# Norm statistics by ScalarE's accumulator, and step sizes whose logarithm stays in PSUM

## The reference

```python
h = _layernorm(x, axis=-1) * (1 + ca) + sa
x = x + ga * _L0_attn_ref(h, ...)        # inside: a second layernorm of h, with a scale and a bias
h = _layernorm(x, axis=-1) * (1 + cb) + sb
x = x + gb * _L0_ffn_ref(h, ...)

# _L0_attn_ref, its core
xn = (x - mu) * rsqrt(var + 1e-05) * norm_scale + norm_bias
xb, z = split(xn @ W_in)
xb = silu(conv3(xb) + conv_b)
dt = softplus(xb @ W_dt + b_dt)
h = exp(dt * A) * h + (dt * x_t) * B_t       # per token, 16 states of 512 channels
y_t = sum_n(h * C_t)
return residual + ((y + D * xb) * silu(z)) @ W_out
```

## Time and profile before

| | us |
|---|---|
| median of three runs | 3125.44 |
| lowest and highest | 3113.62, 3128.53 |
| the profiled execution | 3116.45 |
| its span | 3114.7 |
| a row in the middle of it | 181.1 |
| DVE busy, share of the span | 2638.9, 85% |
| POOL busy | 2623.7, 84% |
| PE busy | 2564.0, 82% |
| ACT busy | 1313.1, 42% |

### The profile page before, as it was taken

How to read it: one execution, slowest core, us unless ns; L and a number is a source line. 1 busy time by engine, 2 the same in 40 slices (tenths; PEclk the granted TensorE clock), 3 DMA queues, 4 the chain that set the end, 5 groups by cost and what they waited for, 6 DMA issues and landing times.

```text
span 3114.7 us, 29047 instructions
## 1 busy us (share of the span) xinstructions
PE 2564.0 (82%) x9260; PEld 1772.5 (57%) x9260; DVE 2638.9 (85%) x3121; ACT 1313.1 (42%) x2081; POOL 2623.7 (84%) x1354
## 2 busy tenths in 40 slices
PE   3435796988979798897979899797988879798879
PEld 1112574656657465665756566574656657465668
DVE  2589898998989899898989998898989989898932
ACT  1434453444445344444534444354444445444311
POOL 0499898989989898998988899898989989898922
PEclk8767898999989898998989899898989989898989
DMA  5234343444434343444434344444434434443411
GB/s 148 75 114 124 120 136 109 130 130 126 146 120 132 114 134 126 131 141 121 136 114 131 124 137 136 119 136 124 132 119 134 133 119 136 122 132 122 149 42 50
DMA packets 282074, 383.40 MB, mean 123 GB/s; under 512 B 44080, under 2 KB 146992, under 8 KB 281920
## 3 DMA queue, kind: packets, MB, share of 16 engines
q1 hardware_dynamic: 281920, 381.54, 40.3%
HBM read 371.38 MB, written 10.06 MB: 122 GB/s over the span
## 4 chain that ended last, share of the span: by engine, by line
PE 33%; POOL 27%; DVE 20%; issue 15%; ACT 4%; SPq 1%; DMA 1%; POOLq 0%; DVEq 0%; ACTq 0%
PE wbank L450 10%; POOL unit L1094 9%; PE mbank L462 6%; DVE hbank L740 5%; POOL act L1082 4%; PE wbank L368 4%; DVE unit L747 4%; PE wbank L478 3%; PE wbank L406 3%; POOL gsum L1114 3%; POOL unit L1109 3%; POOL gsum L1109 2%; DVE st L537 2%; PE wbank L392 2%; POOL dtx L1061 1%
## 5 line engine op out<-in xcount | busy, mean ns | idle before, releaser
L1094 POOL TENSOR_TENSOR unit<-dtx,b_bc 128x1024 f32<-128x1024 f32 x512 | 1213.0, 2371 | 3.6 <-DMA b_bc<-bc_scratch 3.6
L740 DVE TENSOR_TENSOR_SCAN hbank<-hbank,unit 128x1024 f32<-128x1024 f32 x512 | 1172.2, 2290 | 26.0 <-POOL unit L1094 25.5
L973 ACT ACTIVATE hbank<-dt,a_neg 128x512 f32<-128x512 f32 x1024 | 666.6, 681 | 532.3 <-DVE unit L747 484.1
L450 PE MATMUL wbank<-h_t,up_t 128*128 128x256 f32 x2048 | 540.3, 411 | 138.2 <-DVE act L712 68.5
L747 DVE TENSOR_TENSOR unit<-hbank,c_bc 128x1024 f32<-128x1024 f32 x512 | 622.7, 1216 | 18.5 <-DMA c_bc<-bc_scratch 0.7
L450 PEld LDWEIGHTS wbank<-h_t,up_t 128*128 128x128 f32 x2048 | 411.5, 205 | 262.8 <-DVE act L712 74.5
L450 PE MATMUL wbank<-h_t,gate_t 128*128 128x256 f32 x2048 | 519.4, 400 | 48.8 <-DVE gz L594 48.5
L462 PE MATMUL mbank<-down_t,act 128*128 128x256 f32 x2048 | 511.4, 389 | 43.5 <-POOL act L1082 43.3
L1082 POOL TENSOR_TENSOR act<-act,w_all 128x512 f32<-128x512 f32 x256 | 337.3, 1318 | 199.1 <-DVE act L719 199.1
L462 PEld LDWEIGHTS mbank<-down_t,act 128*128 128x128 f32 x2048 | 390.3, 194 | 166.6 <-POOL act L1082 73.4
L450 PEld LDWEIGHTS wbank<-h_t,gate_t 128*128 128x128 f32 x2048 | 411.1, 202 | 115.4 <-DVE gz L594 52.8
(11 more groups left out here) (120 smaller groups left out, 2353.7 us busy)
## 6 DMA issues: line engine op xcount, KB each, us to landing
b_bc<-bc_scratch SPq DMA_DIRECT2D x512, 256.0 KB, 4.4
c_bc<-bc_scratch SPq DMA_DIRECT2D x512, 256.0 KB, 4.3
w_all<-w_scratch SPq DMA_DIRECT2D x256, 256.0 KB, 3.5
ht<-in_L_attn_x_dram SPq DMA_DIRECT2D x16, 512.0 KB, 5.0
xt<-in_L_attn_x_dram SPq DMA_DIRECT2D x16, 512.0 KB, 4.9
out_dram<-xt SPq DMA_DIRECT2D x16, 512.0 KB, 3.3
z<-mod_scratch SPq DMA_DIRECT2D x16, 256.0 KB, 3.4
gsum<-in_L_ffn_gate_proj_dram SPq DMA_DIRECT2D x4, 512.0 KB, 4.3
```

The costliest lines, as they stand in the source:

```text
L450: m = eng.matmul(t.bank[:, j * HT:(j + 1) * HT], w[:, 2 * first + j, k, :], h2_t[:, k, h * HT:(h + 1) * HT], start=k == 0, stop=k == HK - 1)
L740: eng.tensor_tensor_scan(h, h, unit[:, g % RING, :, :].rearrange("p a t -> p (a t)"), 0.0, ALU.mult, ALU.add).then_inc(scanned, 1)
L973: eng.activation(hbank[g % HB][:, a, :], dt[:, 2 * q + a, :], ACT.Exp, scale=a_neg[:, 2 * q + a, n:n + 1]).then_inc(decayed, 1)
L1094: eng.tensor_tensor(unit[:, g % RING, :, :], dtx[:, 2 * q:2 * q + 2, :], b_bc[:, s:s + 1, :].to_broadcast([P, 2, T]), ALU.mult).then_inc(d ...
```

## The change

**Norms.** `norm_stats` goes from DVE. ACT reads the four tiles of a row once with Identity and its accumulator, which gives four sums (`row_sums`; the tile is written back over itself), POOL makes minus the mean of them (`row_means`), ACT reads the tiles again with Square, the bias minus the mean and the accumulator (`row_squares`; the squares themselves go into two tiles of `z2` by turns and are not used), and POOL makes `ve` with one more TENSOR_SCALAR ahead of rstd and shift. A norm thus has eight more ACTIVATE, all with the accumulator, 384 in the 48 norms, and POOL has 96 more TENSOR_SCALAR of 128x4. From DVE go 192 BN_STATS, 192 BN_AGGR and 96 TENSOR_SCALAR. In a norm work now goes ACT, POOL, ACT, POOL, ACT, where it went DVE, POOL, ACT.

**Step sizes.** ACT takes relu into `dt`, then |v|, Exp and Ln in the PSUM bank itself, tile by tile; DVE adds `dt` and the bank per tile (64 of 128x512 where there were 32 of 128x1024) and only that frees the bank. Table loads go from 65 to 129.

**The table.** Stages are cut into other numbers of steps and stand at other moments: `stats` one moment later, `norms` 25 to 37 in 12 steps, `gates` 25 to 42 instead of 19 to 35, `turn_in` from 42, `step_sizes1` 3 to 14 instead of 0 to 5, `mix1` 11 to 12.

```diff
-                plan += [("mix1", behind, 4, 8, 11), ("load_res", behind, 1, 11, 13), ("load_gb", behind, 1, 11, 19),
-                         ("project", behind, 4, 15, 19), ("stats", behind, 4, 18, 19),
-                         ("turn", behind, 4, 23, 27), ("pick", behind, 5, 25, 25), ("weigh", behind, 2, 33, 33)]
-            plan += [("step_sizes1", slot, 9, 0, 5), ("load_ga", slot, 1, 17, 35), ("gates", slot, 9, 19, 35),
+                plan += [("mix1", behind, 4, 11, 12), ("load_res", behind, 1, 0, 12), ("load_gb", behind, 1, 1, 21),
+                         ("project", behind, 4, 15, 19), ("stats", behind, 5, 19, 21),
+                         ("turn", behind, 4, 21, 25), ("pick", behind, 5, 25, 25), ("weigh", behind, 2, 33, 33)]
+            plan += [("step_sizes1", slot, 9, 3, 14), ("load_ga", slot, 1, 37, 38), ("gates", slot, 9, 25, 42),
...
-                plan += [("load_x", coming, 1, 17, 25), ("norms", coming, 9, 28, 37), ("turn_in", coming, 2, 38, 46),
+                plan += [("load_x", coming, 1, 14, 27), ("norms", coming, 12, 25, 37), ("turn_in", coming, 2, 42, 47),
...
+            def row_sums(src, out, done):
+
+                for q in range(TT):
+                    i = eng.activation(src[:, q, :], src[:, q, :], ACT.Identity, accum_out=out[:, q:q + 1])
+                i.then_inc(done, 1)
+
+            def row_squares(src, mean, out, done, at):
+
+                for q in range(TT):
+                    if q >= 2:
+                        need.wait_ge(done, at + q - 1)
+                    eng.activation(z2[:, q % 2, :], src[:, q, :], ACT.Square, bias=mean[:, q:q + 1],
+                                   accum_out=out[:, q:q + 1]).then_inc(done, 1)
...
-                    eng.activation(dtx[:, m_, :], t.bank[:, :], ACT.Abs, bias=b_dt[:, m_:m_ + 1]).then_inc(soft_act, 1)
...
-                    eng.activation(dt[:, m_, :], t.bank[:, :], ACT.Relu, bias=b_dt[:, m_:m_ + 1]).then_inc(t.free, 1)
-                    need.wait_ge(soft_act, at + 2 * n + 1)
-                    eng.activation(dtx[:, m_, :], dtx[:, m_, :], ACT.Exp, scale=-1.0).then_inc(soft_act, 1)
...
-                need.wait_ge(soft_act, at + 4)
-                eng.activation(dtx[:, pair, :], dtx[:, pair, :], ACT.Ln, bias=1.0).then_inc(soft_act, 1)
+                    x = t.bank[:, :]
+                    eng.activation(dt[:, m_, :], x, ACT.Relu, bias=b_dt[:, m_:m_ + 1]).then_inc(soft_act, 1)
+                    eng.activation(x, x, ACT.Abs, bias=b_dt[:, m_:m_ + 1]).then_inc(soft_act, 1)
+                    need.wait_ge(soft_act, at + 2)
+                    eng.activation(x, x, ACT.Exp, scale=-1.0).then_inc(soft_act, 1)
+                    need.wait_ge(soft_act, at + 3)
+                    eng.activation(x, x, ACT.Ln, bias=1.0).then_inc(soft_act, 1)
...
+            def row_means(total, mean, made):
+
+                eng.tensor_scalar(mean[:, :], total[:, :], -1.0 / H, None, ALU.mult).then_inc(made[0], 1)
+
+            def row_scales(total, var_eps, mean, scale, bias, made):
+
+                eng.tensor_scalar(var_eps[:, :], total[:, :], 1.0 / H, EPS, ALU.mult, ALU.add).then_inc(made[0], 1)
+                need.wait_ge(made[0], made[1] + 1)
                 eng.tensor_tensor(scale[:, :], var_eps[:, :], minus_half[:, :], ALU.pow).then_inc(made[0], 1)
...
-                eng.tensor_tensor(dt[:, pair, :], dt[:, pair, :], dtx[:, pair, :], ALU.add).then_inc(dt_made, 1)
+                    eng.tensor_tensor(dt[:, m_, :], dt[:, m_, :], t.bank[:, :], ALU.add).then_inc(t.free, 1)
```

More of the change, by code:

```diff
@@ L613, in project @@
                     yield
[L615 to L622 removed]
             def pick(row):
[L625 removed]
+                at = ROUTE_V * row
                 t = work.at["logits", row]
@@ L838, in norms @@
             def norms(row):
+                h = ht[:, row % 2, :, :]
+                need.wait_ge(x_in, 16 * (row + 1))
+                if row >= 2:
+                    t = work.at["h2", row - 2, HK - 1]
+                    need.wait_ge(t.full, t.after)
+                elif row:
+                    xb_ready(need, row - 1)
+                row_sums(h, sums, norm_a)
+                yield
+                yield
+                need.wait_ge(norm_p, 10 * row + 1)
+                row_squares(h, nmean, squares, norm_a, 10 * row + 1)
+                yield
+                yield
+                need.wait_ge(norm_p, 10 * row + 4)
+                norm_apply(h, h, rstd, shift, normed)
                 yield
@@ L841, in norms @@
                 yield
-                need.wait_ge(norm_p, 6 * row + 2)
-                norm_apply(ht[:, row % 2, :, :], ht[:, row % 2, :, :], rstd, shift, normed)
-                for _ in range(5):
-                    yield
-                need.wait_ge(norm_p, 6 * row + 6)
-                if row >= 2:
-                    t = work.at["h2", row - 2, HK - 1]
-                    need.wait_ge(t.full, t.after)
-                norm_apply(ht[:, row % 2, :, :], z2, rstd, shift, normed)
+                need.wait_ge(norm_p, 10 * row + 6)
+                row_sums(h, sums, norm_a)
+                yield
+                yield
+                need.wait_ge(norm_p, 10 * row + 7)
+                row_squares(h, nmean, squares, norm_a, 10 * row + 6)
+                yield
+                yield
+                need.wait_ge(norm_p, 10 * row + 10)
+                norm_apply(h, z2, rstd, shift, normed)
                 yield
@@ L1048, in norms @@
                 yield
-                need.wait_ge(norm_v, 8 * row + 8)
-                row_scales(mv, ve, rstd, shift, (norm_p, 6 * row + 5))
+                need.wait_ge(norm_a, 10 * row + 6)
+                row_means(sums, nmean, (norm_p, 10 * row + 6))
+                yield
+                yield
+                need.wait_ge(norm_a, 10 * row + 10)
+                row_scales(squares, ve, nmean, rstd, shift, (norm_p, 10 * row + 7))
+                yield
                 yield
@@ L1057, in step_sizes @@
                     yield
-                need.wait_ge(dt_made, 2 * row + q + 1)
+                for m_ in (2 * q, 2 * q + 1):
+                    t = work.at["dt", row, m_]
+                    need.wait_ge(t.free, t.after)
                 xb_ready(need, row)
```

110 lines of the change are left out of this document (42 added, 68 removed).

## The result

The changed kernel takes 3129.53 us (median of 20 runs, 3127.05 to 3131.65), the kernel before on the same chip 3119.23 us (20 runs, 3110.04 to 3128.53): a ratio of 1.0032, 95% interval 1.0024 to 1.0039. It is slower, as forecast, but by 10 us and not by 47. The profiled spans are 3127.7 and 3114.7 us.

A forecast was written before the change was run, and what follows sets the result against it. Each row was taken as a run set by PE plus a chain set by latencies. Chain 33.6 us over 14 slots, 0.9 and 1.5 for slots 0 and 15, ends 11.4: +47 us, 3173 us median, range 3060 to 3245.

The forecast's parts named there:

- Run and chain: A 181.08 us row cut in two: 131.95 us with PE nearly always busy, 49.13 us of engine-to-engine latencies from x1.
- PE sets the run: In the row's 131.95 us stretch PE is busy 128.60 us and sets its length; the change takes nothing from PE.
- the second half of the chain: From DVE's choice of experts to PE's busy stretch: latencies sum to 30.0 us, +0.9, less 0.8 for PE's clock: +0.1.
- DVE's freed time: Pair sums get 1.8 us shorter, 58 us in all; nothing gained, since PE is behind already or DVE waits before the choice.
- First half: From x1 to DVE's choice of experts: 13.93 us before, 14.6 after, +0.7 us a row before any accumulator cost.
- The accumulators: Sum writes by ACT, sixteen of 24 a row on the latency path, 0.1 us each: +1.6 us, bounds 0 to 3.4.
- The slots: Row positions: 14 full ones at +2.4 us, 33.6 in all; slot 0 +0.9, slot 15 +1.5.
- the ends: The start's two norms and the last row's, which nothing covers: +3.8 us each, 11.4 in all.
- Step sizes and bank: PSUM bank held 6.7 us, PE back after 6.9 us; four more table loads a row just fit: counted 0.
- The bank rival: ACT comes late to step-size tiles and PE stalls 1.0 us on each of four: 64 us more, 3237 us; chance 0.13.
- The faster case: DVE, not PE, sets the 131.95 us stretch, which shrinks 3.6 us a row: 3076 us; chance 0.25.
- No change: Accumulators cost nothing, handovers fall into waits, only the uncovered norms at start and end are paid: 3134 us; chance 0.17.

The follow-up runs named there:

- D's products: Changed kernel with the four D products of a row, 3.44 us of PE, left out of the computation: 3095.22 us, 0.9922.
- seven kernels: Changed kernel and variants of it: five or twelve unused PE products, POOL's second-norm scales moved earlier, no third-norm squares, no accumulator reads; 3108.81 to 3129.57 us.
- the early scales: Changed kernel with POOL's second-norm ve, rstd and shift ahead of its drive: 3128.97 us; with twelve unused PE products too: 3114.91 us.
- the accumulators: Changed kernel whose norm sums and squares are made without accumulator reads from the second row on: 3125.51 us, 1.0011.
- the fill: Changed kernel with one more unused DVE reduction, one SBUF operand, behind each tile's sum of step sizes, 64 in all: 3129.3 us, 1.0036.
- the doubled products: Changed kernel with twelve unused PE products, plus `ups2` of the first expert step made two or three times: 3112.25 and 3112.86 us.
- six mixtures: Kernels between before and changed, combining old or new table, DVE or ACT norms, step sizes by pair or tile: 3124.7 to 3165.3 us.

## Why the prediction was wrong in size

- **Run and chain, the step that failed.** The cut held, and so did "PE sets the run" (D's products). But the prediction took the second half of the chain as a sum of latencies, so that each new piece of the norm would lengthen the row, and counted the run as independent of it. The runs show POOL at work without a gap from the choice until 24 us into the run: 50.2 to 50.4 us in seven kernels. Before, POOL had 2.3 us of gaps there, and the norm's new pieces went beside it. What leaves the chain's second half comes back in the run, as with the early scales, and what is added there costs nothing, as with the accumulators. That chain and run together follow POOL there was nowhere in the prediction.
- **DVE's freed time counts nothing.** Right under the table that came with it, by the fill and by a run of 131.85 us. DVE has 117.9 us there instead of 121.9. It would not have been right for the pair's sum under the new table, where 1.4 us a row of DVE's time stand ahead of x1.
- **First half, forecast 15.4 us with accumulators, measured 15.48.** Two errors that cancel. The norm was quicker: apply starts 6.15 us after x1 and not 7.4, since sums come every 0.40 us and squares every 0.49, not every 0.6. The clock took it back: I had the logits at 1.98 us as before, and did not ask what stood ahead of them on PE. After 9.74 us without work and with no `gates` product between, they take 1.59 us more. That the sum came out to a tenth is luck. DVE's idle time ahead of the choice, forecast at 5 us, is 1.53 + 3.48 + 1.01 = 6.0.
- **Second half, forecast +0.9 us with accumulators, measured -1.1.** This is where 2.0 of the 2.1 us lie by which the row was forecast too long. The `gates2` at which my path met PE starts at 19.0 us and not at 20.7, again by the quick sums and squares. The path then went through PE's clock, which the doubled products refute. Up to the run it goes POOL's scales, ACT's apply, tanh of `gates`, DVE's product, scan and `act`; the row as a whole goes by POOL's stretch.
- **The accumulators, +1.6 us a row.** This term's size was wrong as well: 0.37 us. The upper neighbour, an instruction of 0.21 us, was the right one (0.19), but it overlaps the ACTIVATE ahead of it by 0.1 us. That is 0.09 us each, near the 0.1 of the forecast; what failed is that sixteen of them would count. Four do, and the other twelve stand beside POOL's work.
- **The slots.** 14 x 2.4 = 33.6 us forecast for the full rows; -0.7 measured between the two traces, and by the median row +0.25 each, 3.5. That is the miss. Slot 15 cost 3.5 for 1.5, slot 0 2.7 for 0.9, the ends 5.6 + 1.9 = 7.5 for 11.4. The start's two norms alone, without cover, cost 4.0 for 7.6, which is the quick sums and squares once more.
- **Step sizes and bank, 0.** Right for the whole: 64 loads more and no longer run. The bank rival fell, and in this kernel twice the loads cost nothing: with both operands in SBUF the tiles take 3161.65 us and the pair 3165.25. But the tiles cost 9 us under the old table, and the pair would cost 36 under the new one; neither was in the prediction, which took the table as given.
- **Rivals.** The faster case (the run follows DVE) fell with the fill. "No change", accumulators at nothing, handovers in waits and only the ends paid, 3134 us, is nearly what happened, with 0.17: the handovers fell into POOL's work. That POOL might be what they wait beside was not asked, though it has 39.74 us of the chain's 49.13 in the earlier trace rows.

## What to carry to other kernels

A chain through several engines is as long as the fullest list among them allows: before adding up new instructions, look what stands ahead of each receiver (here POOL's drive of 2.35 us), and whether one engine has any gap left in the stretch. New work is hidden beside a full list, and a gain there only moves the wait. When work is moved, look at what it leaves behind: a product gone from an idle stretch of PE made the next ones twice as long. A table of order and the work that it orders are one change: four of the six mixtures were 35 to 46 us slower than the kernel before.

## What the runs showed of the hardware

- A sum by ACT's accumulator is two instructions, the ACTIVATE (404 ns for 128x256 without pointer operands, 497 with one, 590 with two) and the read-out (187 to 190 ns), which together come every 0.40 us (sums) and 0.49 us (squares). The Trainium skill, ScalarE: Activation LUTs, What ACT_TABLE_LOAD costs, has 186 ns + 0.833 a column, and 93 for each pointer operand. The estimates worked out from this page of the Trainium skill are 399, 492 and 585 ns for the ACTIVATE, and the trace agrees.
- After 9.74 us of idle time PE's transposes and logits ran at the lower level (granted clock 0.50, 1.2 GHz), 3.57 us for sixteen products of 128x16 that take 1.96 at the higher one (1.00). Five products in the idle stretch, with 5.45 us of idle time behind them, left the clock at 0.50; with eleven, and 0.30 us, it was 1.00.
- DVE's sum of a tile with both operands in SBUF took 0.68 to 5.5 us beside POOL, with one of them in PSUM never above 0.69.
- A table load takes 1283 ns, and in 127 of 129 cases the next ACTIVATE starts 0.01 us behind it.
